# Rounding the high part of each new state on ScalarE, in front of the error and beta's squash, in an attention and mixture-of-experts kernel

## The chip, the core and the metric

The kernel runs on one core of a Trainium2 chip. The metric is the device time in microseconds (us). Before the change it is 370.67 us, the median of 3 runs (370.46 to 371.39).

## What is computed

The input is 16 sequences of 128 tokens with 128 features. Four parts follow each other, each added to x: an attention that works over the Fourier transform of the sequence, a feed-forward part with composed weights, a softmax cross attention, and a router with experts that moves a state in two iterations. The change lies in the last part:

```python
def _inl(ctrl, x, v, mu):
    alpha_raw, beta_raw, gate_raw = jnp.split(ctrl, 3, axis=-1)
    alpha, beta, gate = sigmoid(alpha_raw), softplus(beta_raw), sigmoid(gate_raw)
    error = x - mu
    v_next = alpha * v - beta * error
    x_next = x + DT * gate * v_next
    return (x_next, v_next)
...
for _ in range(NUM_ITER):                     # 2 iterations
    ctx = concat([integrated, v])
    # shared controls, and those of the 2 chosen experts of 8:
    # gelu(ctx @ w1 + b1) @ w2 + b2, then _inl, then the weighted sum of the three
    halt = sigmoid(gelu(x_next @ w_h1 + b_h1) @ w_h2 + b_h2)
    refined = gelu(x_next @ w_f1 + b_f1) @ w_f2 + b_f2
    integrated = integrated + halt * refined * integration_weight
    v = v_next
```

## The kernel before

Every engine's program is written out by hand, and its order is the order of the code. Engines wait for each other by counting semaphores alone. The 2048 tokens stand in 4 chunks of 512 columns, with the 128 features on the partitions. The first half of the kernel (to about 150 us) makes the composed weights, the layer norms, both attentions and the router. The second half runs the two iterations over the 4 chunks as 8 steps (STEPS), s = 0 to 7; step s works on chunk s % 4, and steps 4 to 7 are the second iteration.

To keep fp32 accuracy with fast matmuls, an operand is split: a high part, the value rounded to the type fp32r, and a low part, the value minus the high part. A product is then three matmuls: high by high, low weights by high, high by low. This is done for the hidden layer's input (x_hi and x_lo, and v_hi and v_lo in the second iteration), for the masked hidden tiles (hm_even and hm_odd), and for the new state xn (x_next of the reference) in front of the refinement and the halt layer: xn_hi and xn_lo.

The steps overlap. In round s of the loops the engines do the following, in this order.

- VectorE: `stepped(s-1)` turns the squashed controls into the new velocity and the new state xn (L1056). `refine(s-2)` takes rr (the refinement's second layer) and th (the tanh of the halt layer), multiplies them into rr (L1077), and adds rr to xi and then xT (L1079, L1081; first iteration) or to the result (L1083; second iteration). `state_next_split(s-1)` makes xn_hi (L1090) and xn_lo (L1092). `hidden_masked(s+1)` masks and splits the hidden tiles of the next step (L855, L871, L873, L876), with the low parts of the next state in between (L887, L890). `halt_low(s-1)` makes the low part of the halt layer's hidden values (L1097).
- ScalarE: the GELUs of the hidden layer of step s+1 (L465, L467, L449, L453); `refine2(s-2)` (L555, L558) makes rr and th; `state_high(s+2)` makes x_hi (L530) and, from s = 2 on, v_hi (L533), which wait for the xi of `refine(s-2)`; `squashed(s, BETA)` first makes ne, the negative error (L571), and then beta's softplus (L577, L578). The GELUs of `refine1(s-1)` (L540) and `halt1(s-1)` (L548, L549) follow, then the squashes of alpha and gate.
- TensorE: the hidden layer of step s+1, the second refinement layer (`refine_b(s-2)`), the controls of beta, then those of alpha or gate with `refine_a(s-1)` and `halt_a(s-1)` in between. All its matmuls here go through one helper (L1124), so they are told apart by their operands: `xn_hi,wf_hi` is the refinement, `xn_hi,wh_hi` the first halt matmul, which is put behind a wait for the first GELU of the refinement.

xn_hi and rr share one buffer, which is why xn_hi may only be written once `refine(s-2)` has read rr: this is what `refined(engine, s-1)` waits for, by the semaphore of xi for the first steps and by that of res for the later ones. ScalarE loads a function table (ACT_TABLE_LOAD, 1.28 us) when it goes from GELU or tanh to softplus, and again on the way back.

After round 7 comes an end in which steps can't overlap: `last_gate` on ScalarE and `last_stepped` on VectorE (L1071 makes the last xn), the split, refinement, halt layer and result of step 7.

Of the kernel before, what the change touches and what calls it, by code (L numbers as in the profile page):

```python
# [51 lines left out]
def build(nc, d_xtok, d_xT, d_ctxT, d_packA, d_packB, d_packC, d_a1, d_b1, d_a2, d_b2, d_out):  # L52
    F, BF, U32 = mybir.dt.float32, mybir.dt.bfloat16, mybir.dt.uint32
    FR = mybir.dt.float32r
    ALU, ACT, AX = mybir.AluOpType, mybir.ActivationFunctionType, mybir.AxisListType
# [6 lines left out]
    with ctx:  # L62
# [5 lines left out]
        def sem(name):  # L68
            if name not in sems:
                sems[name] = ctx.enter_context(nc.semaphore(name))  # L70
            return sems[name]
# [38 lines left out]
        def W(name, a=0, b=None):  # L110
            r, at, n = colB[name]
            return pB[0:r, at + a:at + (n if b is None else b)]
# [111 lines left out]
        def placed(name, cols, at):  # L224
            return nc.alloc_sbuf_tensor_at(name, [128, cols], FR, offset=at)[:, :]
# [9 lines left out]
        xn_hi, xn_lo = placed("xn_hi", CH, ctxT_at + 4 * 3 * CH), placed("xn_lo", CH, zz_at + 4 * 2 * CH)  # L235
# [8 lines left out]
        xn = zz[:, 2 * CH:3 * CH]  # L244
# [4 lines left out]
        def ck(c):  # L249
            return slice(c * CH, (c + 1) * CH)  # L250
# [13 lines left out]
        STEPS = ITER * NCH  # L264
        ALPHA, BETA, GATE = 0, 1, 2

        def parts(s):

            return (BETA, GATE) if s < NCH else (BETA, ALPHA, GATE)
# [5 lines left out]
        def group_of(s, part):  # L275
            return group(s, parts(s).index(part))
# [8 lines left out]
        def group_ps(n):  # L285

            return ps[:, (n % 2) * 3 * CH:(n % 2 + 1) * 3 * CH].rearrange("p (k n) -> p k n", k=3)

        def refined(engine, n):

            engine.wait_ge(sem("xi") if n <= NCH else sem("res"), n if n <= NCH else n - NCH)
# [59 lines left out]
        def _(act):  # L351
# [74 lines left out]
            def second_exp(c, n=1):  # L426

                act.wait_ge(sem("dl"), c + n)
                t = slice(c * BPC, (c + n) * BPC)
                act.activation(rt[:, 6, t], rt[:, 4, t], ACT.Exp).then_inc(sem("de"), 1)  # L430
# [7 lines left out]
            def weights_evac(c, ba, bb):  # L438
                for k in range(2):
                    act.wait_ge(sem("c_ps"), 2 * c + k + 1)  # L440
                    act.activation(cb[:, c, k, :], bank[(ba, bb)[k]][:, :], ACT.Copy).then_inc(sem("cb"), 1)

            def hidden_gelus(s, tiles=range(HT + 1)):
                for j in tiles:
                    act.wait_ge(sem("hid_ps"), 5 * s + j + 1)
                    if j == HT:
                        if s >= 1:
                            act.wait_ge(sem("hsl"), s)
                        act.activation(hs, hid_bank(s, HT), ACT.Gelu, bias=W("bs1")).then_inc(sem("hs"), 1)  # L449
                        if s >= 2:  # L450

                            act.wait_ge(sem("part_ps"), group(s - 1, 0))
                        act.activation(hsh[:, s % 2, :], hid_bank(s, HT), ACT.Gelu, bias=W("bs1"))\  # L453
                            .then_inc(sem("hsu"), 1)
                    else:
                        if s >= 1:
                            act.wait_ge(sem("hm") if j else sem("hlo"), (HT - 1) * (s - 1) + j if j else HT * (s - 1) + 1)
                        if j == 0:
                            if s == 0:
                                act.wait_ge(sem("bp"), 1)  # L460
                                act.wait_ge(sem("ew2_lo"), 2)
                            if s >= 2:

                                act.wait_ge(sem("part_ps"), group(s - 1, 0))
                            act.activation(masked(s)[:, 0, 0, :], hid_bank(s, 0), ACT.Gelu,  # L465
                                           bias=W("eb1", 0, 1)).then_inc(sem("hhi_0"), 1)
                        act.activation(hid[:, j, :], hid_bank(s, j), ACT.Gelu,  # L467
                                       bias=W("eb1", j, j + 1)).then_inc(sem("hid"), 1)
# [55 lines left out]
            def state_high(s):  # L524

                c = s % NCH
                act.wait_ge(sem("hid_ps"), 5 * s)
                if s >= NCH:
                    act.wait_ge(sem("xi"), c + 1)
                act.activation(x_hi, xi[:, ck(c)], ACT.Copy).then_inc(sem("xhi"), 1)  # L530
                if s >= NCH:
                    act.wait_ge(sem("v1"), c + 1)
                    act.activation(v_hi, vT[:, ck(c)], ACT.Copy).then_inc(sem("vhi"), 1)  # L533

            def refine1(s):
                for j in range(2):
                    act.wait_ge(sem("f1_ps"), 2 * s + j + 1)
                    if s >= 1:
                        act.wait_ge(sem("f2_ps"), s)
                    act.activation(fh[:, j, :], bank[7 - j], ACT.Gelu, bias=W("bf1", j, j + 1))\  # L540
                        .then_inc(sem("fhg"), 1)
# [9 lines left out]
            def refine2(s):  # L551
                act.wait_ge(sem("f2_ps"), s + 1)
                if s >= 1:
                    refined(act, s)
                act.activation(rr, bank[7], ACT.Identity, bias=bfi[:, 0:1], scale=iwh[:, 0:1])\  # L555
                    .then_inc(sem("rr"), 1)
                act.wait_ge(sem("h2_ps"), s + 1)
                act.activation(th, bank[6], ACT.Tanh, bias=bh2h[:, 0:1], scale=0.5)\  # L558
                    .then_inc(sem("th"), 1)

            def squashed(s, part):

                n = group_of(s, part)
                if s >= 1:
                    act.wait_ge(sem("xn"), s)
                if part == BETA:
                    if s >= NCH:
                        act.wait_ge(sem("xi"), s % NCH + 1)
                    else:
                        act.wait_ge(sem("z"), LN["rt", s] + 1)  # L570
                    act.activation(ne, xi[:, ck(s % NCH)], ACT.Identity, bias=W("mu"), scale=-1.0)\  # L571
                        .then_inc(sem("ne"), 1)
                act.wait_ge(sem("part_ps"), n + 1)
                out = (al, bg[:, 0], bg[:, 1])[part]
                f, scale, bias = (ACT.Softplus, 1.0, W("bs2", BETA, BETA + 1)) if part == BETA else \
                    (ACT.Tanh, 0.5, bs2h[:, part:part + 1])
                act.activation(out[:, 0], group_ps(n)[:, 0], f, scale=scale, bias=bias).then_inc(sem("squash"), 1)  # L577
                act.activation(out[:, 1:3], group_ps(n)[:, 1:3], f, scale=scale).then_inc(sem("squash"), 1)  # L578

            def last_gate():  # L580

                n = group_of(STEPS - 1, GATE)
                for k in range(3):
                    act.wait_ge(sem("stream_ps"), k + 1)
                    act.activation(bg[:, 1, k], group_ps(n)[:, k, :], ACT.Tanh, scale=0.5,
                                   bias=0.0 if k else bs2h[:, GATE:GATE + 1]).then_inc(sem("stream"), 1)

            act.wait_ge(sem("consts"), 4)
            for s in range(STEPS):
                if s + 1 < STEPS:  # L590
                    hidden_gelus(s + 1)
                if s == 0:
                    second_exp(NCH - 2, 2)
                if s == 1:
                    weights_evac(NCH - 1, 7, 6)
                if s >= 2:
                    refine2(s - 2)
                if s + 2 < STEPS:
                    state_high(s + 2)
                squashed(s, BETA)  # L600
                if s >= 1:
                    refine1(s - 1)
                if s == 0:
                    expand_evac(NCH - 1, 7, 6)
                    weights_evac(NCH - 2, 7, 6)
                if s >= 1:
                    halt1(s - 1)
                squashed(s, parts(s)[1])
                if NCH <= s < STEPS - 1:
                    squashed(s, GATE)  # L610
            refine2(STEPS - 2)
            last_gate()
            refine1(STEPS - 1)
            halt1(STEPS - 1)
            refine2(STEPS - 1)
# [3 lines left out]
        def _(dve):  # L619
# [464 lines left out]

            def state_next_split(s):

                dve.wait_ge(sem("xn"), s + 1)
                if s >= 1:
                    refined(dve, s)
                dve.tensor_copy(xn_hi, xn).then_inc(sem("xnhi"), 1)  # L1090
                dve.wait_ge(sem("xnhi"), s + 1)
                dve.tensor_tensor(xn_lo, xn, xn_hi.bitcast(F), ALU.subtract).then_inc(sem("xnlo"), 1)  # L1092

# [565 lines left out]
```

## Time and profile before

| | |
|---|---|
| median of 3 runs | 370.67 us (370.46 to 371.39) |
| profiled execution, its own time | 368.45 us |
| its span, first to last instruction | 366.7 us |
| TensorE matmul busy | 329.7 us (90%) |
| VectorE busy | 285.3 us (78%) |
| ScalarE busy | 196.7 us (54%) |
| chain that ended last | TensorE 55%, VectorE 25%, issue 11%, ScalarE 4% |
| mean granted TensorE clock | 0.973 of full speed |

A row of a timeline has the start in us, the length in us, the engine, the line of the code, the operation and its output and inputs; brackets hold the idle time before it and what ended it. PE is TensorE (PEld its weight loads), DVE is VectorE, ACT is ScalarE. Names are those of the memory that is used, so xn appears as zz, ne, beta's and gate's controls as kv, rr as ctxT, and th as kv. The granted clock is given as a share of full speed (2.4 GHz), so 0.50 is 1.2 GHz.

### The profile page before, as it was taken

How to read it: one execution, taken by the hardware profiler on the slowest of the kernel's cores; microseconds unless marked ns; L12 is line 12 of the kernel's file. 1: busy time of each engine (PE TensorE's matmuls, PEld its weight loads, DVE VectorE, ACT ScalarE, POOL GpSimd, SP SyncE). 2: the span in 40 equal slices, each digit the busy share in tenths (PEclk: the TensorE clock that was granted, in tenths of full speed). 3: DMA queues.
4: the chain of work that ended last, by engine and by line, in shares of the span. 5: the costliest groups of instructions: out<-in, count | busy, mean ns of one | idle time of the engine just before them, and what ended most of it. 6: DMA issues, size and time to landing. Idle time of an engine off the chain costs nothing.

```text
span 366.7 us, 4373 instructions
## 1 busy us (share of the span) xinstructions
PE 329.7 (90%) x1516; PEld 232.0 (63%) x1516; DVE 285.3 (78%) x596; ACT 196.7 (54%) x306; POOL 17.4 (5%) x20
## 2 busy tenths in 40 slices
PE   4989999898988777997998999999999999998952
PEld 4754886455555555575775776777777777776630
DVE  0556766646867778989999999999998997993952
ACT  2500034485555473396767765866468456538522
POOL 0040011211110102000000000000000000000000
PEclk9989999999999999599999999999999999999988
DMA  7999910000000000000000000000000000000000
GB/s 261 426 414 290 347 70 0 1 1 2 0 0 3 0 0 2 0 2 1 1 2 0 0 0 2 0 2 1 0 1 2 0 0 30 0 0 30 0 29 29
DMA packets 10726, 17.85 MB, mean 49 GB/s; under 512 B 337, under 2 KB 8529, under 8 KB 9425
## 3 DMA queue, kind: packets, MB, share of 16 engines
q1 hardware_dynamic: 10704, 17.58, 13.8%
q8 instruction: 12, 0.20, 0.2%
q14 instruction: 10, 0.07, 0.1%
HBM read 16.53 MB, written 1.05 MB: 48 GB/s over the span
## 4 chain that ended last, share of the span: by engine, by line
PE 55%; DVE 25%; issue 11%; ACT 4%; POOL 2%; DMA 2%; POOLq 1%; ACTq 0%; DVEq 0%; SPq 0%
PE ps L1124 50%; DVE zz L761 3%; DVE lst L746 2%; POOL lrs L347 2%; PE ps L1221 2%; DMA ctxT<-in_ctxT 2%; DVE kv L1048 1%; DVE ring L855 1%; DVE kv L1049 1%; DVE kv L1047 1%; DVE kv L1051 1%; PE ps L1200 1%; DVE st L646 1%; DVE lmv L749 1%; DVE ctxT L1077 1%
## 5 line engine op out<-in xcount | busy, mean ns | idle before, releaser
L1124 PE MATMUL ps<-hm_odd,ew_hi 128*128 128x512 f32 (+1 forms) x169 | 52.8, 417 | 0.0
L1124 PE MATMUL ps<-hm_even,ew_hi 128*128 128x512 f32 (+1 forms) x160 | 49.7, 414 | 0.0
L1124 PEld LDWEIGHTS ps<-hm_odd,ew_hi 128*128 128x128 f32 (+1 forms) x169 | 29.6, 189 | 6.4 <-issue 0.2
L1124 PEld LDWEIGHTS ps<-hm_even,ew_hi 128*128 128x128 f32 (+1 forms) x160 | 27.5, 188 | 5.2
L1124 PE MATMUL ps<-hm_odd,ew_lo 128*128 128x512 f32 (+1 forms) x80 | 28.6, 395 | 0.0
L1124 PE MATMUL ps<-hm_even,ew_lo 128*128 128x512 f32 (+1 forms) x80 | 28.0, 389 | 0.0
L467 ACT ACTIVATE hid<-ps,pB 128x512 f32<-128x512 f32 x32 | 21.8, 688 | 10.4 <-PE ps L1124 9.8
L1124 PE MATMUL ps<-x_hi,w1x_hi 128*128 128x512 f32 x40 | 19.8, 495 | 4.2 <-ACT hid L467 3.9
L761 DVE TENSOR_SCALAR zz<-ps,lmv,lrs 128x128 f32<-128x128 f32 x48 | 16.4, 404 | 7.7 <-POOL lrs L347 7.5
L855 DVE SCALAR_TENSOR_TENSOR ring<-ring,pB,hid 128x1024 f32<-128x1024 bf16 x16 | 20.5, 1282 | 0.9
L746 DVE BATCH_NORM_STATS2 lst<-ps 128x6 f32<-128x128 f32 x48 | 10.7, 285 | 11.9 <-PE ps L1200 11.8
L347 POOL TENSOR_TENSOR lrs<-lve,mhalf 128x4 f32<-128x4 f32 x12 | 13.1, 1089 | 107.2 <-DVE lve L751 107.2
L1124 PE MATMUL ps<-zz,pB 128*128 128x512 f32 x32 | 15.3, 599 | 2.2 <-DVE h1s L1097 2.2
L1124 PE MATMUL ps<-ring,a 128*128 128x512 f32 x32 | 16.0, 653 | 1.0 <-DVE a L662 1.0
L1124 PE MATMUL ps<-x_hi,w1x_lo 128*128 128x512 f32 x40 | 16.7, 416 | 0.0
L1124 PE MATMUL ps<-x_lo,w1x_hi 128*128 128x512 f32 x40 | 16.5, 412 | 0.0
L1124 PEld LDWEIGHTS ps<-hm_odd,ew_lo 128*128 128x128 f32 (+1 forms) x80 | 13.9, 188 | 2.9
L1124 PE MATMUL ps<-zz,wz 128*128 128x512 f32 x32 | 15.6, 596 | 0.0
L1124 PEld LDWEIGHTS ps<-hm_even,ew_lo 128*128 128x128 f32 (+1 forms) x80 | 13.7, 188 | 2.7
L578 ACT ACTIVATE kv<-ps 128x1024 f32<-128x1024 f32 x15 | 15.3, 1018 | 0.0
L1124 PEld LDWEIGHTS ps<-b,ring 128*128 128x128 f32 x128 | 14.7, 192 | 0.6 <-issue 0.5
L1124 PE MATMUL ps<-b,ring 128*128 128x128 f32 x128 | 15.0, 276 | 0.0
(272 smaller groups left out, 749.3 us busy)
## 6 DMA issues: line engine op xcount, KB each, us to landing
ring<-in_fc1b SPq DMA_DIRECT2D x4, 1024.0 KB, 17.4
ring<-in_fc2a SPq DMA_DIRECT2D x4, 1024.0 KB, 8.4
packC<-in_packC SPq DMA_DIRECT2D x1, 1152.0 KB, 9.4
pB<-in_packB SPq DMA_DIRECT2D x1, 1125.5 KB, 9.9
ctxT<-in_ctxT SPq DMA_DIRECT2D x2, 512.0 KB, 6.5
xtok<-in_xtok SPq DMA_DIRECT2D x1, 1024.0 KB, 9.1
xT<-in_xT SPq DMA_DIRECT2D x1, 1024.0 KB, 11.1
a<-in_fc1a SPq DMA_DIRECT2D x1, 1024.0 KB, 13.1
```

The costliest lines, as they stand in the source:

```text
L347: pool.tensor_tensor(lrs[:, n % 2, :], lve[:, n % 2, :], mhalf[:, 0:BPC], ALU.pow)\
L467: act.activation(hid[:, j, :], hid_bank(s, j), ACT.Gelu, bias=W("eb1", j, j + 1)).then_inc(sem("hid"), 1)
L578: act.activation(out[:, 1:3], group_ps(n)[:, 1:3], f, scale=scale).then_inc(sem("squash"), 1)
L646: dve.bn_stats(st[:, b, :], xtok[:, b, :]).then_inc(sem("st"), 1)
L746: dve.bn_stats(lst[:, n % 2, j, :], t[:, j * D:(j + 1) * D]).then_inc(sem("lst"), 1)
L749: dve.bn_aggr(lmv[:, n % 2, j, :], lst[:, n % 2, j, :]).then_inc(sem("lmv"), 1)
L761: dve.tensor_scalar(ztok[:, n % 2, j, :], t[:, j * D:(j + 1) * D], lmv[:, n % 2, j, 0:1], lrs[:, n % 2, j:j + 1], ALU.subtract, ALU.mult)\
L855: dve.scalar_tensor_tensor(hm[j % 2], idx[:, c, :, :], W("tile_expert", j, j + 1), hid[:, j, :].unsqueeze(1).to_broadcast([128, 2, CH]), A ...
L1047: link(dve.tensor_tensor(bg[:, 0, 1:3], bg[:, 0, 1:3], cb[:, c], ALU.mult))
L1048: link(dve.scalar_tensor_tensor(bg[:, 1], bg[:, 1], 1.0, bg[:, 0], ALU.add, ALU.mult))
L1124: return pe.matmul(out, lhsT, rhs, start=start, stop=stop)
L1221: last = pe.transpose(bank[6][:, j * 128:(j + 1) * 128], ztok[:, n % 2, j, :], ident)
```

## The change

The copy that rounds xn to xn_hi goes from VectorE to ScalarE. There it is a function of its own, with the same waits, called behind `state_high(s+2)` and in front of `squashed(s, BETA)`, and for the last step behind `last_gate`. VectorE's `state_next_split` keeps only the subtraction, which waits for the semaphore of xn_hi as before; that semaphore is now raised by ScalarE.

```diff
--- before.py
+++ after.py
@@ -558,6 +558,13 @@
                 act.activation(th, bank[6], ACT.Tanh, bias=bh2h[:, 0:1], scale=0.5)\
                     .then_inc(sem("th"), 1)
 
+            def state_next_high(s):
+
+                act.wait_ge(sem("xn"), s + 1)
+                if s >= 1:
+                    refined(act, s)
+                act.activation(xn_hi, xn, ACT.Copy).then_inc(sem("xnhi"), 1)
+
             def squashed(s, part):
 
                 n = group_of(s, part)
@@ -597,6 +604,8 @@
                     refine2(s - 2)
                 if s + 2 < STEPS:
                     state_high(s + 2)
+                if s >= 1:
+                    state_next_high(s - 1)
                 squashed(s, BETA)
                 if s >= 1:
                     refine1(s - 1)
@@ -610,6 +619,7 @@
                     squashed(s, GATE)
             refine2(STEPS - 2)
             last_gate()
+            state_next_high(STEPS - 1)
             refine1(STEPS - 1)
             halt1(STEPS - 1)
             refine2(STEPS - 1)
@@ -1084,10 +1094,6 @@
 
             def state_next_split(s):
 
-                dve.wait_ge(sem("xn"), s + 1)
-                if s >= 1:
-                    refined(dve, s)
-                dve.tensor_copy(xn_hi, xn).then_inc(sem("xnhi"), 1)
                 dve.wait_ge(sem("xnhi"), s + 1)
                 dve.tensor_tensor(xn_lo, xn, xn_hi.bitcast(F), ALU.subtract).then_inc(sem("xnlo"), 1)
```

ScalarE in round 2 before, from the second refinement layer on (each row: line, operation, output and inputs, shape, and the semaphores it waits for):

```order
L555 ACTIVATE ctxT<-ps,bfi,iwh 128x512 [waits f2_ps]
L558 ACTIVATE kv<-ps,bh2h 128x512 [waits h2_ps]
L530 ACTIVATE x_hi<-xi 128x512 [waits xi,hid_ps]
L533 ACTIVATE v_hi<-a 128x512 [waits v1]
L571 ACTIVATE kv<-xi,pB 128x512 [waits z,xn]
L577 ACT_TABLE_LOAD
L577 ACTIVATE kv<-ps,pB 128x512 [waits part_ps]
L578 ACTIVATE kv<-ps 128x1024
L540 ACT_TABLE_LOAD [waits f2_ps]
L540 ACTIVATE zz<-ps,pB 128x512 [waits f1_ps]
```

The same place with the change (lines below the new function are numbered 7 higher):

```order
L530 ACTIVATE x_hi<-xi 128x512 [waits xi,hid_ps]
L533 ACTIVATE v_hi<-a 128x512 [waits v1]
L566 ACTIVATE xn_hi<-zz 128x512 [waits xi,xn]
L578 ACTIVATE kv<-xi,pB 128x512 [waits z,xn]
L584 ACT_TABLE_LOAD
L584 ACTIVATE kv<-ps,pB 128x512 [waits part_ps]
```

The copy stands third in a row of copies, in front of ne, and waits for xi as well as xn. No table load is added. In round 7 there is no state_high, and the copy stands directly in front of ne and waits for res:

```order
L555 ACTIVATE ctxT<-ps,bfi,iwh 128x512 [waits res,f2_ps]
L558 ACTIVATE kv<-ps,bh2h 128x512 [waits h2_ps]
L566 ACTIVATE xn_hi<-zz 128x512 [waits res,xn]
L578 ACTIVATE kv<-xi,pB 128x512 [waits xi,xn]
L584 ACT_TABLE_LOAD
```

VectorE in round 2 before, from the new state to the first mask:

```order
L1056 SCALAR_TENSOR_TENSOR zz<-kv,xi 128x512 [waits h1_ps,dve_chain]
L1077 SCALAR_TENSOR_TENSOR ctxT<-kv,ctxT 128x512 [waits th,rr]
L1079 TENSOR_TENSOR xi<-xi,ctxT 128x512 [waits dve_chain]
L1081 TENSOR_TENSOR xT<-xT,xi 128x512 [waits xi]
L1090 CAST xn_hi<-zz 128x512 [waits xi,xn,dve_chain]
L1092 TENSOR_TENSOR xn_lo<-zz,xn_hi 128x512 [waits xnhi]
L855 SCALAR_TENSOR_TENSOR ring<-ring,pB,hid 128x1024 [waits hlo,idx,hid]
```

And with the change (lines numbered 10 higher up to the new state, 6 higher at xn_lo):

```order
L1066 SCALAR_TENSOR_TENSOR zz<-kv,xi 128x512 [waits h1_ps,dve_chain]
L1087 SCALAR_TENSOR_TENSOR ctxT<-kv,ctxT 128x512 [waits th,rr]
L1089 TENSOR_TENSOR xi<-xi,ctxT 128x512 [waits dve_chain]
L1091 TENSOR_TENSOR xT<-xT,xi 128x512 [waits xi]
L1098 TENSOR_TENSOR xn_lo<-zz,xn_hi 128x512 [waits xnhi,dve_chain]
L865 SCALAR_TENSOR_TENSOR ring<-ring,pB,hid 128x1024 [waits hlo,idx,hid]
```

The cast is gone, and xn_lo waits for another engine, with all masks of the round queued behind it.

## Rows read from the trace of the kernel before

**Rows 1.** Chain that ended last, in order of time (start us, us, what), 170 us to the end:

```profile
249.48 0.70 DVE xi L1079
...
256.27 0.70 ACT zz L540
...
257.01 74.92 PE ps L1124 x332
```

**Rows 2.** Timeline of VectorE (start us, us, instruction, [idle before <-releaser]), round 1 and start of 2:

```profile
180.65 0.69 DVE L1092 TENSOR_TENSOR xn_lo<-zz,xn_hi 128x512 fp32r<-128x512 f32 x1
...
193.87 1.23 DVE L1047 TENSOR_TENSOR kv<-kv,hB 128x1024 f32<-128x1024 f32 x1 [0.39 <-ACT kv L578]
```

**Rows 3.** Timeline of ScalarE, round 1:

```profile
181.58 0.72 ACT L571 ACTIVATE kv<-xi,pB 128x512 f32<-128x512 f32 x1
...
184.11 0.69 ACT L577 ACTIVATE kv<-ps,pB 128x512 f32<-128x512 f32 x1 [0.51 <-PE ps L1124]
```

**Rows 4.** Timeline of VectorE, round 2:

```profile
202.16 0.69 DVE L1079 TENSOR_TENSOR xi<-xi,ctxT 128x512 f32<-128x512 f32 x1
...
203.62 0.43 DVE L1090 CAST xn_hi<-zz 128x512 fp32r<-128x512 f32 x1
...
204.08 0.69 DVE L1092 TENSOR_TENSOR xn_lo<-zz,xn_hi 128x512 fp32r<-128x512 f32 x1
```

**Rows 5.** Timeline of ScalarE, round 2:

```profile
202.95 0.63 ACT L530 ACTIVATE x_hi<-xi 128x512 fp32r<-128x512 f32 x1 [2.18 <-DVE xi L1079]
...
204.01 0.71 ACT L571 ACTIVATE kv<-xi,pB 128x512 f32<-128x512 f32 x1
...
208.95 1.27 ACT L540 ACTIVATE zz<-ps,pB 128x512 f32<-128x512 f32 x2
```

**Rows 6.** Timeline of TensorE, halt matmul of round 2:

```profile
210.00 0.39 PE L1124 MATMUL ps<-xn_hi,wh_hi 128*128 128x512 f32 x1
```

**Rows 7.** Timeline of ScalarE, rounds 5 and 6:

```profile
283.99 1.27 ACT L540 ACTIVATE zz<-ps,pB 128x512 f32<-128x512 f32 x2
...
309.61 0.69 ACT L577 ACTIVATE kv<-ps,pB 128x512 f32<-128x512 f32 x1 [2.50 <-PE ps L1124]
```

**Rows 8.** Timeline of TensorE, halt matmul of round 5:

```profile
285.82 0.39 PE L1124 MATMUL ps<-xn_hi,wh_hi 128*128 128x512 f32 x1
```

**Rows 9.** Timeline of VectorE, round 6:

```profile
305.29 0.69 DVE L1077 SCALAR_TENSOR_TENSOR ctxT<-kv,ctxT 128x512 f32<-128x512 f32 x1 [2.09 <-ACT kv L558]
...
306.02 0.69 DVE L1083 TENSOR_TENSOR xT<-xT,ctxT 128x512 f32<-128x512 f32 x1
...
307.28 0.69 DVE L1092 TENSOR_TENSOR xn_lo<-zz,xn_hi 128x512 fp32r<-128x512 f32 x1
```

**Rows 10.** Timeline of ScalarE, round 7:

```profile
330.20 0.72 ACT L571 ACTIVATE kv<-xi,pB 128x512 f32<-128x512 f32 x1 [3.96 <-DVE zz L1056]
...
335.15 1.27 ACT L540 ACTIVATE zz<-ps,pB 128x512 f32<-128x512 f32 x2
```

**Rows 11.** Timeline of VectorE, round 7:

```profile
330.81 0.69 DVE L1083 TENSOR_TENSOR xT<-xT,ctxT 128x512 f32<-128x512 f32 x1
...
332.06 0.69 DVE L1092 TENSOR_TENSOR xn_lo<-zz,xn_hi 128x512 fp32r<-128x512 f32 x1
```

**Rows 12.** Timeline of TensorE, halt matmul of round 7 and first matmul after it ends:

```profile
336.67 0.40 PE L1124 MATMUL ps<-xn_hi,wh_hi 128*128 128x512 f32 x1
...
353.28 0.47 PE L1124 MATMUL ps<-xn_hi,wf_hi 128*128 128x512 f32 x1 [3.41 <-issue]
```

**Rows 13.** Timeline of VectorE, end of last_stepped:

```profile
351.30 0.69 DVE L1071 SCALAR_TENSOR_TENSOR zz<-kv 128x512 f32<-128x512 f32 x1
...
352.49 0.69 DVE L1092 TENSOR_TENSOR xn_lo<-zz,xn_hi 128x512 fp32r<-128x512 f32 x1
```

**Rows 14.** Stretches: busy us of PE, PEld, DVE, ACT, POOL; granted clock; DMA share, GB/s:

```profile
172.00:176.00 4.00, 1.35 (x6) 1.04 (x6) 3.87 (x5) 3.49 (x6) 0.00 (x0) 1.00 0.00 0
...
354.00:355.00 1.00, 1.00 (x3) 0.79 (x3) 0.00 (x0) 0.55 (x1) 0.00 (x0) 0.50 0.00 0
```

## The prediction

> **Names.** The last phase runs in rounds s = 0 to 7. In round s VectorE finishes the new state of step s-1 (stepped), finishes the refinement of step s-2 (refine), splits the new state of step s-1 into xn_hi and xn_lo, and then masks the hidden tiles of step s+1. ScalarE and TensorE have their own part of the round. All times are those of the profiled execution.
>
> **What bounds the kernel now.** I first read the chain of waits from the back. Up to about 192 us it runs over TensorE. From 194 to 250 us (rounds 2 to 4) it is VectorE alone, ending in the addition that makes xi in round 4. It then goes over ScalarE (the first GELU of the refinement) to TensorE, and stays there for 75 us [rows 1]. So a delay of VectorE in rounds 2 to 4 is worth its full length. Later, TensorE and what it waits for decide, and the last 14 us are a chain of single instructions.
>
> Next I read the timelines of the three engines side by side, round by round, because what the change is worth depends on who stands in front of the moved copy on ScalarE.
>
> **What is removed.** Eight VectorE casts of 128x512, each 0.43 us and 0.46 us from start to start of the next [rows 4]. If the ScalarE copy were always there in time, that would be the gain of a round.
>
> **What is added.** Eight ScalarE copies of the same shape. The same operation exists already: x_hi<-xi takes 0.63 us, and x_hi and v_hi together hold back what stands behind them by 204.01 - 202.95 = 1.06 us, so one copy costs a successor 0.53 us [rows 5]. I take 0.54. The Trainium skill ("ScalarE: Activation LUTs", section "Rules for kernel authors") speaks against the move: it sends simple elementwise work to VectorE and budgets about 0.3 us plus 0.83 ns per element for an ACTIVATE, 0.73 us for 512 by that rule (an estimate from the page); with 0.73 in place of 0.63 each of the waits below would be 0.1 us longer, and the sum about 0.5 us larger. The row of this case is 0.63, so the sum goes without it.
>
> The copy is not only slower: it stands behind x_hi and v_hi in ScalarE's order, and these two wait for xi, which VectorE makes two instructions before it wants xn_hi. So VectorE now waits for three copies. From VectorE to ScalarE I take 0.10 us (xi ends at 202.85, x_hi starts at 202.95 [rows 4, 5]); for the way back I take 0.06 us, between nothing and that 0.10.
>
> **Round 1.** No xi is waited for. On ScalarE, x_hi stands in front, and the new copy takes the place where ne (kv<-xi) starts now, 181.58 [rows 3]. It ends at 182.21, so xn_lo starts at 182.27 instead of 180.65 [rows 2]: VectorE is 1.62 us later. The tanh and softplus work behind it on ScalarE hardly moves, since softplus waited 0.51 us for TensorE [rows 3]. VectorE had 0.39 us of idle time before 193.87, which the delay uses up: it is ready 1.62 us later than 193.48, and with the usual 0.03 to the next instruction it starts at 195.13 [rows 2]. Shift of VectorE: +1.26.
>
> **Round 2.** xi, x_hi and v_hi come 1.26 later. The copy starts where ne started, 204.01, ends at 204.64, and xn_lo can start at 204.70 against 204.08 before [rows 4, 5]: +0.62 on top. VectorE is at +1.88. ScalarE's chain behind the copy (ne, table load, softplus, table load, GELU) ran without a gap, so the GELU at 208.95 comes 1.26 + 0.54 = 1.80 later; it ends (0.69 us for one) near 211.44, and TensorE, which used its result for the halt matmul at 210.00, waits until 211.5: TensorE at +1.5 [rows 5, 6].
>
> **Round 3.** VectorE +0.62 again, now +2.50. ScalarE's GELU at +1.88 + 0.54 = +2.42; TensorE's halt matmul waits for it as in round 2, so TensorE is at about +2.4.
>
> **Round 4.** xi at +2.50, the GELU at 256.27 at +2.50 + 0.54 = +3.04, and TensorE at 257.01, which waited for it [rows 1], at +3.04. VectorE at +3.12. Terms so far: 1.26 + 0.62 + 0.62 + 0.54 = 3.04 us.
>
> **Rounds 5 and 6.** TensorE is busy without a gap and keeps +3.04. In round 5 the GELU stands at +3.04 + 0.54 and ends (0.69 us after 283.99) at 288.26; the halt matmul wants it at 285.82 + 3.04 = 288.86 [rows 7, 8]. Hidden, with 0.6 us to spare. In round 6 VectorE waits for the tanh of ScalarE (2.09 us before 305.29) and is back at TensorE's +3.04; the copy now also waits for the res addition, which ends at 306.71 + 3.04 = 309.75. Copy from 309.85 to 310.48, xn_lo at 310.54 against 307.28: VectorE at +3.26 [rows 9]. On ScalarE ne used to run at 305.08, early. Now ne, the table load (1.28 us) and softplus come behind the copy: 310.39, 311.11, softplus at 312.4. Softplus had waited 2.50 us for TensorE until 309.61, with the shift 312.65 [rows 7]. Hidden, with 0.2 us to spare.
>
> **Round 7.** Here it isn't hidden. ne waited only for xn, and started at 330.20, while res was made 330.81 to 331.50 [rows 10, 11]. With the change the copy stands in front of ne and waits for res: 331.50 + 3.26 + 0.10 = 334.86. ne starts at 335.40, 5.20 later than before. The chain from there to the GELU at 335.15 is without a gap, so the GELU is at +5.20 and ends at 341.04; TensorE's halt matmul of this round, at 336.67 before, follows 0.05 us later (as at 257.01 [rows 1]): TensorE goes from +3.04 to +4.42 [rows 10, 12]. That is a term of 1.38 us. Everything after it (the last controls, VectorE's last_stepped) hangs on TensorE here.
>
> **The end.** In last_stepped xn ends at 351.99 and xn_lo starts at 352.49 [rows 13]. With the copy on ScalarE: 352.09 to 352.72, xn_lo at 352.78: +0.29, straight on the end chain (TensorE stands idle there for 3.41 us [rows 12]). No function-table load is added, since none stands between last_gate and the refinement's GELU in the new order either.
>
> Sum: 3.04 + 1.38 + 0.29 = 4.71 us. The profiled execution takes 368.45 us (span 366.7), so it would be 373.2. The median of the runs is 370.67, 2.2 above the profiled time, and I add the same 4.7: **375.4 us**, 1.3% slower. About 0.3% is what a measurement of this kernel can tell from no change.
>
> **Rivals.**
> 1. *The cast is simply gone from VectorE (faster).* Place: the three rounds where VectorE is the chain. It decides if the three ScalarE copies end before VectorE has ended the xT addition at about 203.6; they would have to start 1.1 us earlier than 202.95 [rows 4, 5]. Then rounds 2 and 3 give 2 x 0.46 = 0.9 us, less 0.29 at the end: 370.1 us, within the noise; with a third round counted 369.6. Against it: x_hi waits for xi, made only 0.77 us before xn_hi is wanted. Chance 2%.
> 2. *Round 7 is milder.* If the GELU did not hold TensorE there, only xn_lo would: it starts at 334.86 + 0.63 + 0.06 = 335.55 against 332.06 [rows 11], +3.49 for TensorE, and the sum is 3.49 + 0.29 = 3.8: 374.5 us. For it: the matmuls before the halt matmul gave 0.8 us of cover. Against it: ScalarE would have to be 0.9 us faster than its unbroken chain. Chance 13%.
> 3. *The clock helps or hurts.* The granted clock is 1.00 nearly throughout, also over the gap of 172 to 176 us with TensorE busy 1.35 of 4 us; it was 0.50 in 354 to 355 us, after the idle 3.41 us [rows 12, 14]. Nine matmuls stand there, 0.43 us apart (half the clock, 1.2 GHz) where 0.23 is usual. If the fall comes elsewhere than on them: about -1.4, 374.0 us; chance 12%. If it also falls on the gaps of about 1 us that rounds 2 and 7 now have, or on the refinement's second layer: +1 to +2, 376.4 to 377.4 us; chance 8%. The Trainium skill ("TensorE: Matmul & The Clock Gate", Part 1) says that the moment of the change of clock varies from run to run; the rows here show one execution, so they can't say.
>
> **How the numbers follow.** Forecast 63%, rival 2 13%, rival 3 20% in its two directions, rival 1 2%, and 2% that some slack I didn't see swallows nearly all. The likeliest case has its own range of 374.8 to 376.0, from the way back (0.00 to 0.10 us, five times) and the 0.2 us of cover in round 6. The range for 8 in 10 is 373.9 to 376.5. Slower by over 0.3% (above 371.8) in all cases but the last two: 0.96; within 0.3% 0.03; faster 0.01.
>
> **What would show it.** Right: VectorE idle before xn_lo in every round, released by ScalarE's xn_hi; about 2.1 us in round 1 and 1.1 us in rounds 2 to 4 (the delays of 1.62 and 0.62 plus the cast's 0.46); TensorE idle about 1 us before the halt matmul of rounds 2 and 7; ne in round 7 started by the copy, not by xn. Wrong: the three copies done before the xT addition ends, or the halt matmul of round 7 released by something else than the GELU, or the chain of waits in rounds 2 to 4 no longer on VectorE and its wait for xn_hi.

## The result, and the profile after

The change makes the kernel slower: 374.95 us median (374.76 to 375.14, 5 runs) against 370.67 (370.15 to 371.39, 5 runs), a ratio of 1.0113, 95% interval 1.0099 to 1.0127. The prediction said 375.4. The profiled execution takes 374.77 us with a span of 372.6, 5.9 us more than the span before. About 1.5 us of that come from TensorE's clock at the end, which differs between executions of one kernel, as will be seen.

The waits of the kernel after, from 178 us to the end (engine and instruction, what it waited for, us in total, times, longest):

```profile
DVE xn_lo L1098 <- ACT xn_hi L566: 10.0, 8, 3.3
...
ACT xn_hi L566 <- DVE xT L1093: 7.2, 2, 5.5
```

VectorE waits for the copy all eight times, 10.0 us in total. In two rounds (6 and 7) the copy itself waits for the addition that makes res, which is the xT of L1093. VectorE (timeline) in rounds 1 and 2, to be held against [rows 2, 4], and at the end, against [rows 13]:

```profile
182.11 0.69 DVE L1098 TENSOR_TENSOR xn_lo<-zz,xn_hi 128x512 fp32r<-128x512 f32 x1 [3.25 <-ACT xn_hi L566]
...
203.24 0.69 DVE L1089 TENSOR_TENSOR xi<-xi,ctxT 128x512 f32<-128x512 f32 x1
203.97 0.69 DVE L1091 TENSOR_TENSOR xT<-xT,xi 128x512 f32<-128x512 f32 x1
205.81 0.69 DVE L1098 TENSOR_TENSOR xn_lo<-zz,xn_hi 128x512 fp32r<-128x512 f32 x1 [1.14 <-ACT xn_hi L566]
...
356.96 0.69 DVE L1098 TENSOR_TENSOR xn_lo<-zz,xn_hi 128x512 fp32r<-128x512 f32 x1 [0.69 <-ACT xn_hi L566]
```

and on ScalarE, against [rows 5]:

```profile
180.93 0.63 ACT L530 ACTIVATE x_hi<-xi 128x512 fp32r<-128x512 f32 x1
...
204.03 0.63 ACT L530 ACTIVATE x_hi<-xi 128x512 fp32r<-128x512 f32 x1 [3.41 <-DVE xi L1089]
204.57 0.61 ACT L533 ACTIVATE v_hi<-a 128x512 fp32r<-128x512 f32 x1
205.09 0.62 ACT L566 ACTIVATE xn_hi<-zz 128x512 fp32r<-128x512 f32 x1
205.61 0.71 ACT L578 ACTIVATE kv<-xi,pB 128x512 f32<-128x512 f32 x1
...
210.55 1.27 ACT L540 ACTIVATE zz<-ps,pB 128x512 f32<-128x512 f32 x2
```

The three copies x_hi, v_hi, xn_hi run one behind the other from 204.03 to 205.71; VectorE has ended the xT addition at 204.66 and stands idle 1.14 us. The copy takes 0.62 us and holds back ne by 0.52.

Round 7 on ScalarE, against [rows 10]:

```profile
334.65 0.63 ACT L566 ACTIVATE xn_hi<-zz 128x512 fp32r<-128x512 f32 x1 [5.54 <-DVE xT L1093]
335.19 0.71 ACT L578 ACTIVATE kv<-xi,pB 128x512 f32<-128x512 f32 x1
...
340.12 1.27 ACT L540 ACTIVATE zz<-ps,pB 128x512 f32<-128x512 f32 x2
```

and TensorE: the halt matmuls of rounds 2, 4, 5 and 7 and the end, against [rows 6, 8, 12]:

```profile
211.29 0.51 PE L1130 MATMUL ps<-xn_hi,wh_hi 128*128 128x512 f32 x1 [0.78 <-ACT zz L540]
...
259.91 0.50 PE L1130 MATMUL ps<-xn_hi,wh_hi 128*128 128x512 f32 x1 [0.79 <-ACT zz L540]
...
288.69 0.39 PE L1130 MATMUL ps<-xn_hi,wh_hi 128*128 128x512 f32 x1
...
336.10 0.48 PE L1130 MATMUL ps<-xn_hi,wf_hi 128*128 128x512 f32 x1 [1.31 <-issue]
...
340.86 0.50 PE L1130 MATMUL ps<-xn_hi,wh_hi 128*128 128x512 f32 x1 [0.80 <-ACT zz L540]
...
357.76 0.48 PE L1130 MATMUL ps<-xn_hi,wf_hi 128*128 128x512 f32 x1 [3.59 <-issue]
...
363.29 3.75 PE L1130 MATMUL ps<-zz,pB 128*128 128x512 f32 x4 [2.16 <-DVE h1s L1103]
```

The halt matmuls of rounds 2, 4 and 7 wait 0.8 us for the GELU, that of round 5 waits for nothing. The last row is the second refinement layer of the last step: four matmuls take 3.75 us. In the profiled execution before the same four took 1.95 us:

```profile
359.13 1.95 PE L1124 MATMUL ps<-zz,pB 128*128 128x512 f32 x4 [2.16 <-DVE h1s L1097]
```

The granted clock says why (stretches; the columns are those of [rows 14]). After, in the first layer (359 to 360 us) and in the second (364 to 365 us):

```profile
359.00:360.00 1.00, 1.00 (x3) 0.52 (x3) 0.00 (x0) 0.65 (x2) 0.00 (x0) 0.50 0.00 0
364.00:365.00 1.00, 1.00 (x2) 0.34 (x1) 0.00 (x0) 0.00 (x0) 0.00 (x0) 0.50 0.00 0
```

Before, in the second layer:

```profile
360.00:361.00 1.00, 1.00 (x4) 0.38 (x2) 0.00 (x0) 0.00 (x0) 0.00 (x0) 1.00 0.00 0
```

So before, half the clock (1.2 GHz) held for a part of the first layer alone, after for a part of the first and for the second too. The second layer takes 1.80 us longer after, the nine matmuls of the first 0.32 us less (3.37 against 3.69). Together that is 1.5 us of the 5.9. The kernel before has such differences between its own executions: on one chip 28 of them took 367.8 to 371.9 us, with a mean clock of 0.974 to 0.958, and the profiled one is 2.2 us below the median of its kernel.

To follow the shift round by round, the start of an execution has to be taken out: ScalarE makes x_hi of round 1 at 180.93 after and at 181.06 before:

```profile
181.06 0.63 ACT L530 ACTIVATE x_hi<-xi 128x512 fp32r<-128x512 f32 x1
```

With 0.13 us added, the shifts are:

| place | predicted | measured |
|---|---|---|
| xn_lo of round 1 (182.11) | +1.62 | +1.59 |
| xn_lo of round 2 (205.81) | +1.88 | +1.86 |
| GELU of round 2 (210.55) | +1.80 | +1.73 |
| halt matmul of round 2 (211.29) | +1.5 | +1.42 |
| halt matmul of round 4 (259.91) | +3.04 | +3.03 |
| halt matmul of round 5 (288.69) | +3.04 | +3.00 |
| ne of round 7 (335.19) | +5.20 | +5.12 |
| halt matmul of round 7 (340.86) | +4.42 | +4.32 |
| last xn_lo (356.96) | +4.71 | +4.60 |

### The profile page after: what moved, and what is told of

The parts are those of the page before. It is cut to its first block, busy times and chain, and to the rows that moved or that the text cites. A ratio compares the mean times of both kernels' runs of the same rounds, so it can differ in the third digit from the quotient of the medians.

```text
span 372.6 us, 4369 instructions
## 1 busy us (share of the span) xinstructions
PE 331.1 (89%) x1508; PEld 231.6 (62%) x1516; DVE 281.8 (76%) x588; ACT 201.0 (54%) x314; POOL 17.4 (5%) x20
## 3 DMA queue, kind: packets, MB, share of 16 engines
HBM read 16.53 MB, written 1.05 MB: 47 GB/s over the span
## 4 chain that ended last, share of the span: by engine, by line
PE 41%; DVE 34%; issue 13%; ACT 7%; POOL 2%; DMA 2%; POOLq 1%; ACTq 0%; DVEq 0%; SPq 0%
PE ps L1130 37%; DVE zz L771 3%; DVE ring L865 3%; DVE lst L756 2%; POOL lrs L347 2%; DVE wz L865 2%; DMA ctxT<-in_ctxT 2%; PE ps L1227 1%; DVE kv L1058 1%; DVE hm_even L881 1%; DVE hm_even L883 1%; DVE ctxT L1087 1%; DVE kv L1059 1%; DVE hm_odd L881 1%; DVE kv L1061 1%
## 5 line engine op out<-in xcount | busy, mean ns | idle before, releaser
L1130 PE MATMUL ps<-zz,pB 128*128 128x512 f32 x32 | 17.0, 659 | 2.2 <-DVE h1s L1103 2.2
```

Source lines behind the costliest of these rows:

```text
L1130: return pe.matmul(out, lhsT, rhs, start=start, stop=stop)
```

## The experiments

All of them start from one kernel in which a tuple says which states are rounded on ScalarE; for the others the cast is where it was, on VectorE. Ratios are against the kernel before in runs on the same chip (medians 370.4 to 370.7 us). A difference in us behind a ratio is worked out from it, and not from the two medians, which can be further apart (3.05 us in e6, where the ratio gives 2.4).

```diff
+        HIGH_ON_ACT = (...)
...
             def state_next_high(s):
+                if s not in HIGH_ON_ACT:
+                    return
...
             def state_next_split(s):
+                if s not in HIGH_ON_ACT:
+                    dve.wait_ge(sem("xn"), s + 1)
+                    if s >= 1:
+                        refined(dve, s)
+                    dve.tensor_copy(xn_hi, xn).then_inc(sem("xnhi"), 1)
```

**One part of the rounds at a time.** The first three runs take the change apart by rounds, and ask whether the cost is what is waited for in each, or a flat 0.54 us per copy.

```diff
+        HIGH_ON_ACT = (0,)        # e1_first_only
+        HIGH_ON_ACT = (1, 2, 3)   # e2_mid_only
+        HIGH_ON_ACT = (6, 7)      # e3_late_only
```

> Only the state of step 0 (round 1) is rounded on ScalarE, the other seven on VectorE as before. Waiting theory (each round costs what VectorE or TensorE waits for the copy there): xn_lo of round 1 is 1.6 us late, 0.39 us of it is swallowed by VectorE's idle time, and +1.2 us stay to the end: 371.9 us. Rival (each moved copy costs its 0.54 us on ScalarE, in whatever round): +0.5 us, 371.2 us.

Measured: 371.24 us, ratio 1.0027 (1.0009 to 1.0046), +0.3 to +1.7 us. This interval holds both theories; the trace decides. xn_lo of round 1 waits for the copy, and the halt matmul of round 4 (257.01 before) is 1.23 us late, once the later start (0.82 us) is taken out:

```profile
183.06 0.69 DVE L1107 TENSOR_TENSOR xn_lo<-zz,xn_hi 128x512 fp32r<-128x512 f32 x1 [3.44 <-ACT xn_hi L570]
```

```profile
259.06 0.50 PE L1139 MATMUL ps<-xn_hi,wh_hi 128*128 128x512 f32 x1 [0.60 <-ACT zz L542]
```

> Only the states of steps 1 to 3 (rounds 2 to 4) are rounded on ScalarE. Waiting theory: VectorE waits 1.1 us before xn_lo in each round where the cast took 0.46, +0.62 in rounds 2 and 3, and ScalarE's chain to the GELU +0.54 in round 4: +1.8 us, 372.4 us. Rival (0.54 us per copy): +1.6 us, 372.3 us; told apart by the trace alone: it has no wait of VectorE that grows the shift by 0.62 a round.

Measured: 372.46 us, ratio 1.0051 (1.0033 to 1.0070), +1.9 us. VectorE (timeline) waits as expected in all three rounds, and not in round 1:

```profile
179.87 0.69 DVE L1107 TENSOR_TENSOR xn_lo<-zz,xn_hi 128x512 fp32r<-128x512 f32 x1
...
204.88 0.69 DVE L1107 TENSOR_TENSOR xn_lo<-zz,xn_hi 128x512 fp32r<-128x512 f32 x1 [1.15 <-ACT xn_hi L570]
...
229.18 0.69 DVE L1107 TENSOR_TENSOR xn_lo<-zz,xn_hi 128x512 fp32r<-128x512 f32 x1 [1.14 <-ACT xn_hi L570]
...
253.50 0.69 DVE L1107 TENSOR_TENSOR xn_lo<-zz,xn_hi 128x512 fp32r<-128x512 f32 x1 [1.15 <-ACT xn_hi L570]
```

Against the kernel before, and less the later start (0.17 us), xn_lo is 0.63 us late in round 2, 1.27 in round 3 and 1.93 in round 4: it grows by about 0.62 a round, as the waiting theory has it.

> Only the states of steps 6 and 7 (round 7 and the end) are rounded on ScalarE. Waiting theory: in round 7 ne waits for res instead of xn, 1.9 us later, 0.8 us of it are covered, and TensorE's halt matmul is 1.1 to 1.2 us late; at the end 0.3 us: +1.4 us, 372.1 us. Rival (0.54 us per copy): +0.8 us from ScalarE's work, of which round 7's part is covered by the 0.8 us: +0.3 us, 371.0 us.

Measured: 371.89 us, ratio 1.0040 (1.0021 to 1.0060), +1.5 us against +1.4 and the rival's +0.3 (371.0), which lies outside the interval. ScalarE and TensorE in round 7:

```profile
331.73 0.63 ACT L570 ACTIVATE xn_hi<-zz 128x512 fp32r<-128x512 f32 x1 [5.35 <-DVE xT L1097]
332.26 0.71 ACT L582 ACTIVATE kv<-xi,pB 128x512 f32<-128x512 f32 x1
```

```profile
337.94 0.50 PE L1139 MATMUL ps<-xn_hi,wh_hi 128*128 128x512 f32 x1 [0.80 <-ACT zz L542]
```

Nothing is late before round 7 here (its halt matmul of round 4 is at 257.17, with the later start 0.01 us off), and yet TensorE waits 0.80 us for the GELU.

From the traces, each less the difference of its start (0.82, 0.17, 0.17 us; 0.13 added for the change):

| rounds on ScalarE | halt matmul of round 4 | of round 7 | last xn_lo |
|---|---|---|---|
| 1 | +1.23 | +1.22 | +1.22 |
| 2 to 4 | +1.80 | +1.75 | +1.75 |
| 7 and the end | -0.01 | +1.10 | +1.39 |
| all (the change) | +3.03 | +4.32 | +4.60 |

The three parts add up to 4.36 us of the 4.60. The rest of 0.24 is near the 0.22 us that the prediction has VectorE fall behind TensorE in round 6 and hand on to round 7; it was not run alone. The flat price per copy falls: one copy costs 1.2 us in round 1 where it would be 0.54, and two cost 1.4 in round 7 and the end. In rounds 2 to 4 three copies cost 1.8, near 3 x 0.54 = 1.6; there the growing delay of xn_lo speaks against it.

**The place in ScalarE's order.**

```diff
-                if s + 2 < STEPS:
-                    state_high(s + 2)
                 if s >= 1:
                     state_next_high(s - 1)
+                if s + 2 < STEPS:
+                    state_high(s + 2)
```

> All eight copies on ScalarE as in the change, but the copy stands in front of state_high (x_hi, v_hi) instead of behind it. Waiting theory: xn_lo in rounds 2 to 4 can start 0.79 us after xi, about when VectorE has ended the xT addition, so VectorE's waits of 1.1 us there shrink to under 0.1; round 1 still costs 0.7 us and round 7 (no state_high there) about 1.4, the end 0.3: +2.1 us, 372.8 us. Rival (the copies' time on ScalarE is what costs, the place is no matter, since the GELU has all three copies in front of it either way): +4.3 us, 375.0 us, as the change.

Measured: 372.75 us, ratio 1.0064 (1.0043 to 1.0086), +2.4 us, where the change has +4.3. ScalarE does the same work; only the order of copies is another one. xn_lo of round 2 stands 0.10 us behind the xT addition:

```profile
203.00 0.69 DVE L1093 TENSOR_TENSOR xi<-xi,ctxT 128x512 f32<-128x512 f32 x1
203.73 0.69 DVE L1095 TENSOR_TENSOR xT<-xT,xi 128x512 f32<-128x512 f32 x1
204.52 0.69 DVE L1107 TENSOR_TENSOR xn_lo<-zz,xn_hi 128x512 fp32r<-128x512 f32 x1
```

The last xn_lo is 2.14 us later than before (354.74; its start, less the 0.54 us that the copy now holds back x_hi of round 1, was 0.11 later), against the 2.1 expected. TensorE shows where the rest sits (its halt matmuls of rounds 4 and 7):

```profile
257.58 0.50 PE L1139 MATMUL ps<-xn_hi,wh_hi 128*128 128x512 f32 x1 [0.28 <-ACT zz L542]
...
338.62 0.50 PE L1139 MATMUL ps<-xn_hi,wh_hi 128*128 128x512 f32 x1 [0.80 <-ACT zz L542]
```

They are 0.46 and 1.84 us late. Through rounds 2 to 4 VectorE no longer loses 0.62 us a round but gains 0.39 (xn_lo is 0.33 us late in round 2, 0.06 early in round 3, 0.45 early in round 4), so its loss there was the wait behind x_hi and v_hi. What the copy takes on ScalarE is not free either: in round 4 it still stands in front of the GELU, and TensorE is 0.46 us late though VectorE is not. Round 7 (1.38 us) and the end (0.30) cost what they cost in the change. The parts that the expectation names (0.7, 1.4 and 0.3) add up to 2.4, more than its 2.1; the gain of rounds 2 and 3 that makes up for it is not named there.

**The dependence.** xn_hi may not be written before refine has read rr, since they share memory. The next kernels put xn_hi into a part of packA that is dead by then (for state 0 behind the last transposes that use the identity next to it; a cast on VectorE waits for their semaphore, c_ps), and the copy waits for xn alone. They also have the order of e4; own memory with the copy behind state_high was not run.

```diff
-        xn_hi, xn_lo = placed("xn_hi", CH, ctxT_at + 4 * 3 * CH), placed(...)
+        xn_hi, xn_lo = placed("xn_hi", CH, pA_at + 4 * CH), placed(...)
...
             def state_next_high(s):
                 act.wait_ge(sem("xn"), s + 1)
-                if s >= 1:
-                    refined(act, s)
...
             def state_next_split(s):
                 if s not in HIGH_ON_ACT:
                     dve.wait_ge(sem("xn"), s + 1)
-                    if s >= 1:
-                        refined(dve, s)
+                    if s == 0:
+                        dve.wait_ge(sem("c_ps"), 2 * NCH)
...
+        HIGH_ON_ACT = (0, 1, 2, 3, 4, 5, 6, 7)   # e5, with the order of e4
+        HIGH_ON_ACT = (1, 2, 3, 4, 5, 6)         # e6, the same
```

> All eight copies on ScalarE, in front of state_high, and xn_hi in memory of its own (a dead part of packA) instead of rr's, so that the copy waits for xn alone and not for xi or res. Waiting theory: in rounds 2 to 7 the copy runs while VectorE does refine, VectorE waits for nothing before xn_lo, and neither x_hi nor ne of rounds 2 to 6 is held up; round 1 still costs 0.8 us (ScalarE is busy with the weights), the end 0.3 us, and rounds 2 and 3 give 0.46 us each: within 0.5 us of the kernel before, 370.4 us, over 4 us below the change. Rival (ScalarE's own work is what costs): +2 us or more.

Measured: 369.86 us, ratio 0.9989 (0.9967 to 1.0012): no difference from the kernel before, and the rival's +2 us is out. All eight copies are on ScalarE, and the loss is gone. The last xn_lo, 352.49 before, is 0.83 us earlier, taken as for e4 (a start 0.84 us later):

```profile
352.50 0.69 DVE L1105 TENSOR_TENSOR xn_lo<-zz,xn_hi 128x512 fp32r<-128x512 f32 x1 [0.70 <-ACT xn_hi L568]
```

> As the kernel with xn_hi in its own memory, but the states of steps 0 and 7 are rounded on VectorE, where no other work covers the copy. Waiting theory: rounds 2 and 3 give 0.46 us each, round 7 about 0.2, nothing is lost elsewhere: -1.1 us against the kernel before, 369.3 us. Rival: ScalarE's work costs, slower than before.

Measured: 367.65 us, ratio 0.9936 (0.9914 to 0.9957), -2.4 us (-3.2 to -1.6), more than the -1.1 expected. ScalarE in round 7 shows the copy right behind xn, and VectorE has no wait there:

```profile
329.33 0.64 ACT L568 ACTIVATE xn_hi<-zz 128x512 fp32r<-128x512 f32 x1 [3.31 <-DVE zz L1068]
329.87 0.71 ACT L580 ACTIVATE kv<-xi,pB 128x512 f32<-128x512 f32 x1
```

```profile
329.93 0.69 DVE L1095 TENSOR_TENSOR xT<-xT,ctxT 128x512 f32<-128x512 f32 x1
330.54 0.69 DVE L1105 TENSOR_TENSOR xn_lo<-zz,xn_hi 128x512 fp32r<-128x512 f32 x1
```

The last xn_lo is 1.71 us earlier than before (351.47 against 352.49, and a start 0.69 us later). The expectation had counted the cast's slot in rounds 2 and 3 and 0.2 us in round 7. The first part came out: the halt matmuls of rounds 4, 5 and 6 are 0.88 to 0.91 us early. The other was too small: that of round 7 is 1.81 us early. The first matmul of the refinement there needs xn_lo, which ended at 332.75 before; TensorE stood idle 0.93 us and began 0.11 us later. With VectorE ahead of TensorE by the casts it no longer makes, that idle time is gone; the kernel before and this one:

```profile
332.86 0.47 PE L1124 MATMUL ps<-xn_hi,wf_hi 128*128 128x512 f32 x1 [0.93 <-issue]
```

```profile
331.64 0.50 PE L1137 MATMUL ps<-xn_hi,wf_hi 128*128 128x512 f32 x1
```

The interval reaches to that 1.7; whether the rest is the clock at the end wasn't settled.

**The clock at the end.**

```diff
-            for k in range(9):
+            for k in range(22):
                 mm(bank[0], ew2_hi[:, 0:D], masked(STEPS - 1)[:, 0, 1, :])
```

> The kernel before (all casts on VectorE), with 22 instead of 9 dummy matmuls (results unused) in front of the last refinement, about 3 us more of TensorE work in the 3.4 us for which it stands idle. Theory that the clock in the end moves the time by a us or two from one execution to the next: the clock stays 1.00 over the last nine matmuls, -1.4 us, and up to -3 us where the second layer had been slow too: 368.5 us, with less spread. Rival (clock is no matter there, or the dummies hold back the refinement): no change or slower.

Measured: 368.81 us, ratio 0.9957 (0.9939 to 0.9976), -1.6 us, so the clock matters there. The first matmul of the refinement starts where it did before (353.91, less a start 0.62 us later, against 353.28), so the dummies don't hold it back, and the nine matmuls of the first layer take 2.68 us instead of 3.69. The spread is still 2.8 us (367.1 to 369.9, 12 runs, against 367.9 to 371.6 in 29 runs before): the first layer now runs at full clock, the second can still fall. Two stretches of the profiled execution:

```profile
354.00:356.00 2.00, 1.92 (x8) 1.26 (x9) 0.00 (x0) 1.10 (x2) 0.00 (x0) 1.00 0.00 0
360.00:362.00 2.00, 2.00 (x4) 0.75 (x3) 0.00 (x0) 0.00 (x0) 0.00 (x0) 0.56 0.00 0
```

> The kernel with xn_hi in its own memory and states 0 and 7 on VectorE, and 22 dummy matmuls in the end. If both theories hold the gains add: -1.1 and -2 us, 367.3 us, the fastest of all. If one fails, what is left is the other's gain.

Measured: 366.57 us, ratio 0.9896 (0.9873 to 0.9919), -3.9 us. The gains add (2.4 and 1.6), and this version beats both kernels.

> The change (all eight copies on ScalarE, behind state_high), with 22 instead of 9 dummy matmuls in front of the last refinement, so that the clock does not fall on the last nine matmuls. Waiting theory: what the copy costs does not depend on the clock at the end: 4.7 us above the kernel before with the same 22 dummies, 368.8 + 4.7 = 373.5 us. Rival: the clock at the end took part in the change's cost (the measured 4.3, or the 5.9 us between the profiled spans), and the difference is then clearly another one.

> The kernel before with 22 dummy matmuls, once more, on the same chip as the others: 1.5 to 2 us below the kernel before, and 4.7 us below the change with 22 dummies.

Measured: 373.64 us with the copies on ScalarE (ratio 1.0082, 1.0055 to 1.0110) and 368.84 us with the casts on VectorE (0.9964, 0.9941 to 0.9987): 4.8 us between the medians, 4.4 by the ratios, where 4.7 was expected. The second of them is the kernel of e7 once more, and comes out the same (0.9957 there). Each interval is 1 us wide to either side, so the times alone can't tell 4.8 from 4.3. The traces can. The first matmul of the last refinement in the one (e9_fill_after), and in the other (e10_fill_before_again):

```profile
358.01 0.48 PE L1139 MATMUL ps<-xn_hi,wf_hi 128*128 128x512 f32 x1 [0.57 <-issue]
```

```profile
353.17 0.47 PE L1139 MATMUL ps<-xn_hi,wf_hi 128*128 128x512 f32 x1 [0.37 <-issue]
```

358.01 - 353.17 = 4.84, less 0.12 for the start (x_hi of round 1 at 181.09 and 180.97): 4.72 us, with the clock at 1.00 up to there and the first layer taking 2.68 us in both. Only behind it do the two profiles differ by the clock again: the second layer takes 3.42 us in e9 and 1.95 in e10.

> xn_hi in its own memory, states 0 and 7 on VectorE, 22 dummies in front of the last refinement, and 8 more behind its halt matmuls, in the 2.16 us gap before the second layer. If the clock sometimes falls on the second layer (3.5 us instead of 1.95 in some executions), this takes that away: 0 to 1 us below the kernel without the 8, 366.0 us. Rival: no change, 366.6 us; if the dummies delay the second layer, slower.

```diff
             halt_a(STEPS - 1)
+            for k in range(8):
+                mm(bank[0], ew2_hi[:, 0:D], masked(STEPS - 1)[:, 0, 1, :])
             refine_b(STEPS - 1)
```

Measured: 366.66 us, ratio 0.9894 (0.9872 to 0.9916), against 0.9896 for the kernel without the 8 (366.57): no gain is seen, but the interval of 0.8 us to either side holds the expected 0.6 as well as nothing. The traces can't tell, since the second layer takes 1.96 us in the one and took 1.95 in the other. It starts 0.06 us later (357.27 against 356.43, less a start 0.78 us later), so the 8 dummies don't hold it back.

## Why the prediction was right

The time is 0.4 us below the forecast of 375.4, and the terms of the sum can be followed one by one.

- *Round 1* (1.26 us): alone it shifts TensorE by 1.23 in the trace. Right. Only the wait itself was another one, 3.25 us instead of 2.1, since VectorE reached it earlier in this execution. This costs nothing: the end of the wait is set by ScalarE.
- *Rounds 2 to 4* (0.62 + 0.62 + 0.54 = 1.78 us): alone 1.80 in the trace. Right, with waits of 1.14 and 1.15 us where 1.1 was said. The slot in front of x_hi turns VectorE's part of it into a gain and leaves the 0.54 us of ScalarE in round 4 (e4). TensorE's wait was foretold in one piece, about 1 us before the halt matmul; it came in two, 0.78 us there and 0.40 before the refinement, which needs xn_lo.
- *Rounds 5 and 6* (hidden): right. Softplus of round 6 still waited 0.25 us for TensorE, where 0.2 us of cover was said:

```profile
312.48 0.69 ACT L584 ACTIVATE kv<-ps,pB 128x512 f32<-128x512 f32 x1 [0.25 <-PE ps L1130]
```

- *Round 7* (1.38 us): 4.32 - 3.00 = 1.32 in the trace. Right in mechanism and size: with round 7 and the end alone it is 1.10, and the other 0.2 fits VectorE's lag in round 6. Rival 2, which let xn_lo alone set TensorE there, is out: TensorE does wait for xn_lo first (336.10, 1.31 us idle where it was 0.93; 3.37 us late, where the rival said 3.49), and then 0.80 us more for the GELU, which makes it 4.32.
- *The end* (0.29 us): 4.60 - 4.32 = 0.28.
- *Rival 1* (a gain): it needed the three copies to be done at the end of the xT addition; they ended 1.05 us later. Its price was wrong too: it counted rounds 2 and 3 and the end, and left out rounds 1 and 7. In e4 VectorE does have xn_hi in time in rounds 2 to 4, and the kernel is still 2.4 us slower than before. A gain came only once the dependence on rr's memory was cut as well and states 0 and 7 were left on VectorE (e6).
- *Rival 3* (the clock): its mechanism is real, but it was filed as a way in which the change could end, where it is a difference between executions of any of these kernels. Its first size was misread: of the nine matmuls of the first layer before, only those from the fourth on stand 0.43 us apart, and at full clock the nine take 1.0 us less (2.68 in e7 against 3.69), not 1.4. Its second size, 1 to 2 us if the second layer falls too, was met by the profiled execution after (1.80). The gaps of rounds 2 and 7 brought no fall: from 180 to 358 us the granted clock after is 1.00. The clock at the end is the likely reason that the medians are 4.3 us apart where the shift in the traces is 4.6 to 4.7. If a usual execution before has the second layer slow as well, the two kernels differ by the shift of 4.60 less the 0.32 us that the first layer took less after: 4.28, an estimate from the two traces. No profile of such an execution before was taken, so this stays a likely reason and not a shown one.
- *The number.* That 375.4 is near rests on the sum, whose terms hold one by one in the traces (4.71 foretold, 4.60 found). That the medians, 4.28 us apart, are as near to it is in part luck, since the clock at the end by itself moves single times by 1 to 3 us.

## What to carry to other kernels

Before an operation is moved to a less busy engine, ask what stands in front of it in that engine's order, and what those wait for: 54% busy on ScalarE did not say what the move would cost, since the slot given to the copy was behind two others that waited for a result made 0.8 us before the copy was needed. A wait that is carried along for the sake of shared memory (here rr's) must be weighed for what stands behind it too: it delayed ne in round 7 by nearly 2 us (1.89 in e3) though ne does not need it. In this kernel it paid to give the buffer its own memory, to put the copy where ScalarE is idle, and to leave the first and the last cast of the pipeline, which nothing covers, on VectorE.

## What the runs showed of the hardware

- A ScalarE copy of 128x512 fp32 takes 0.62 us and holds back the next by 0.52; VectorE's cast of the same shape takes 0.43 and 0.46. The Trainium skill ("ScalarE: Activation LUTs", "What ACT_TABLE_LOAD costs") gives 186 ns + 0.833 ns per element for an ACTIVATE with immediate scale and bias, and an overlap of about 93 ns back to back. For 512 elements that is 0.61 us, and 0.52 to the next (estimates from the page), and this case agrees. The budget of 0.73 us in the prediction is stated there for a bias that is a pointer operand, which the copy does not have.
- The four matmuls of the last layer took 1.95 us in four of the 13 profiled executions (before, e8, e10, e11) and 3.1 to 3.75 in the other nine, with a granted clock of 1.00 in the kernel before and of 0.50 in the kernel after. Each kernel has one profile, but single times of the kernel before alone range over 4 us (367.8 to 371.9). Dummy matmuls in the idle time before the last refinement gave 1.6 us.
